# Selective-scan block and coupled feed-forward on one core: the product u moved from GpSimd to VectorE, four more state-and-C products moved the other way, and a new set of places

## The reference, cut to what matters

```python
xi, res = split(x @ W_in.T + b_in)              # 512 channels each
xi      = silu(causal_conv4(xi) + b_conv)       # depthwise, 4 taps, along the 1024 tokens
delta   = softplus(xi @ W_x[:512].T + b_x)      # 512 channels
B, C    = xi @ W_x[512:].T + b_x                # 16 states each
h[t]    = exp(delta[t] * A) * h[t-1] + delta[t] * B[t] * xi[t]    # 512 channels x 16 states
y       = sum over states of h * C + xi * D
x1      = layernorm(x + (y * silu(res)) @ W_out.T + b_out)
# three cycles: t = net(out); out = out + coupling(t) * twist(out); then layernorm(x1 + out)
```

## Time and profile before

| | value |
|---|---|
| median of 3 runs | 4040.12 us |
| profiled execution | 4040.28 us, span 4038.5 us |
| GpSimd busy | 3644.6 us, 90% |
| TensorE busy | 3524.4 us, 87%, granted clock 0.946 over the span |
| VectorE busy | 3429.6 us, 85% |
| ScalarE busy | 2959.0 us, 73% |
| DMA queue of SyncE | 47.0% of 16 engines' span |

### The profile page before, as it was taken

The page is one execution under the profiler, slowest core; times in us unless marked ns, Lnnn a source line. Parts: engine busy times, 40 slices in busy tenths (PEclk is TensorE's granted clock), DMA queues, the critical chain, the costliest instruction groups (busy, mean ns, idle before and its releaser), DMA issues. The chain is left out here.

```text
span 4038.5 us, 51729 instructions
## 1 busy us (share of the span) xinstructions
PE 3524.4 (87%) x18776; PEld 1611.5 (40%) x18776; DVE 3429.6 (85%) x2508; ACT 2959.0 (73%) x3918; POOL 3644.6 (90%) x1604
## 2 busy tenths in 40 slices
PE   7669989899998998989898998989989898897766
PEld 3224353443434344353443434344353443434233
DVE  4988988889898898989889898898989889898861
ACT  4447868778786877868777786877868777785753
POOL 4999999999999999999999999999999999999860
PEclk9779999999999999999999999999999999998888
DMA  5354373543536354373644546454363544546320
GB/s 182 130 175 154 128 230 120 188 152 130 186 130 224 129 191 138 122 229 120 197 148 155 159 152 200 140 187 129 133 218 123 194 149 158 160 138 199 127 86 31
DMA packets 329645, 630.04 MB, mean 156 GB/s; under 512 B 27952, under 2 KB 226608, under 8 KB 329136
## 3 DMA queue, kind: packets, MB, share of 16 engines
q1 hardware_dynamic: 329392, 626.74, 47.0%
HBM read 456.76 MB, written 169.87 MB: 155 GB/s over the span
## 5 line engine op out<-in xcount | busy, mean ns | idle before, releaser
L1060 POOL TENSOR_TENSOR work<-u_q,b_quad 128x1024 f32<-128x1024 f32 x1024 | 2397.3, 2372 | 138.2 <-DMA u_q<-u_scratch 97.1
L816 ACT ACTIVATE da<-delta_q,neg_a 128x1024 f32<-128x1024 f32 x1024 | 1126.3, 1112 | 600.9 <-DVE work L995 430.8
L987 DVE TENSOR_TENSOR_SCAN da<-da,work 128x1024 f32<-128x1024 f32 x608 | 1389.9, 2286 | 151.4 <-ACT da L816 119.7
L1067 POOL TENSOR_TENSOR work<-work,c_quad 128x1024 f32<-128x1024 f32 x416 | 985.2, 2368 | 11.6 <-DVE work L987 11.3
L987 DVE TENSOR_TENSOR_SCAN work<-da,work 128x1024 f32<-128x1024 f32 x416 | 945.9, 2278 | 29.9 <-ACT da L816 28.1
L727 PE MATMUL y_sum<-work,v_all 128*32 128x256 f32 x8192 | 613.3, 399 | 303.3 <-POOL work L1067 190.7
L995 DVE TENSOR_TENSOR work<-da,c_quad 128x1024 f32<-128x1024 f32 x608 | 743.9, 1224 | 28.6 <-DMA c_quad<-bc_scratch 4.6
L752 ACT ACT_TABLE_LOAD x563 | 722.3, 1283 | 14.5 <-DMA v_all<-in_vectors 3.9
L727 PEld LDWEIGHTS y_sum<-work,v_all 128*32 128x32 f32 x8192 | 199.8, 110 | 771.0 <-issue 259.3
L613 PE MATMUL banks<-xi,w_all 128*128 128x512 f32 x1024 | 479.8, 612 | 9.4 <-ACT g_act L797 5.1
L600 PE MATMUL banks<-xi,taps 128*128 128x512 f32 x984 | 453.2, 606 | 0.0
(11 more groups left out here) (86 smaller groups left out, 3270.3 us busy)
## 6 DMA issues: line engine op xcount, KB each, us to landing
delta_q<-delta_scratch SPq DMA_DIRECT2D x256, 512.0 KB, 5.8
u_q<-u_scratch SPq DMA_DIRECT2D x256, 512.0 KB, 6.1
delta_scratch<-delta SPq DMA_DIRECT2D x64, 512.0 KB, 2.9
u_scratch<-soft SPq DMA_DIRECT2D x64, 512.0 KB, 2.9
b_quad<-bc_scratch SPq DMA_DIRECT2D x64, 512.0 KB, 4.7
c_quad<-bc_scratch SPq DMA_DIRECT2D x64, 512.0 KB, 7.1
s_quad<-res_scratch SPq DMA_DIRECT2D x128, 256.0 KB, 4.1
y_scratch<-s_quad SPq DMA_DIRECT2D x128, 256.0 KB, 3.2
```

What stands on the lines that cost most here:

```text
L816: act.activation(da[:, t % 2, :], delta_q[:, slot, :], ACT.Exp, scale=neg_a[:, t % PERIOD:t % PERIOD + 1]).then_inc(da_ready, 1)
L987: dve.tensor_tensor_scan(dst, da[:, t % 2, :], work[:, slot, :], 0.0, ALU.mult, ALU.add) \
L1060: pool.tensor_tensor(work[:, slot, :], u_q[:, copied, :], b_quad[:, j, :], ALU.mult) \
L1067: pool.tensor_tensor(work[:, un % WORK, :], work[:, un % WORK, :], c_quad[:, un % PHASE, :], ALU.mult) \
```

## The change

- `u` is made by VectorE, behind each half of delta (128 x 512, twice a block), with both inputs in SBUF. `store_u` waits for both halves. GpSimd's instruction L1082 goes.
- `POOL_AT` has 30 units instead of 26, most of them others than before. VectorE makes 34 products of a batch instead of 38.
- The first convolution: VectorE makes blocks 0, 1, 2 and a half of block 3, TensorE one half.
- New places for nearly all side work; `DELTA_AT`, `BC_AT`, `G_AT` and `CYCLE_AT` stay.

```diff
-POOL_AT = (1, 4, 6, 8, 9, 10, 11, 12, 16, 18, 21, 24, 28, 32, 33, 36, 42, 44, 49, 52, 55, 56, 58, 59, 60, 61)
+POOL_AT = (0, 1, 4, 8, 9, 10, 12, 13, 16, 17, 20, 22, 25, 26, 28, 32, 33, 37, 38, 42, 45, 46, 48, 49, 52, 56, 57, 59, 60, 61)
-X_AT = (0, 0, 19, 24, 37, 37, 45, 49)
-V_AT = (2, 3, 27, 29, 41, 41, 53, 52)
-RES_AT = (0, 1, 26, 26, 36, 39, 47, 50)
+X_AT = (0, 1, 18, 24, 37, 37, 40, 48)
+V_AT = (2, 2, 28, 28, 41, 42, 52, 50)
+RES_AT = (0, 1, 26, 27, 36, 39, 46, 51)
-O_AT = (5, 9, 10, 12)
-T_AT = (15, 15, 15, 15)
+O_AT = (4, 10, 11, 12)
+T_AT = (15, 15, 15, 16)
-F_AT = (-1, 0, 1, 2, 4, 5, 6, 9, 10, 10)
+F_AT = (0, 0, 0, 2, 4, 5, 6, 8, 10, 10)
-E_AT = (57, 58, 59, 61)
+E_AT = (58, 58, 60, 61)
-DELTA_TAKE, DELTA_MAX, U_LAG = 3, 3, 6
+DELTA_TAKE, DELTA_MAX = 3, 3
-MULT_AT, UPD_AT = 11, 14
-DST_AT, UST_AT = (7, 5, 10, 8), (11, 5, 8, 9)
-DLD_AT, ULD_AT = (12, 13, 18, 19), (12, 13, 17, 20)
-SLD, YST = -1, 0
-YGLD_AT = (2, 4, 4, 8)
-RESST_AT = (4, 28, 47, 61)
-X1ST_AT = (15, 16)
-RES_IN_AT = 28
-XRES_AT = 66
+MULT_AT, UPD_AT = 11, 15
+DST_AT, UST_AT = (8, 10, 6, 9), (8, 4, 4, 8)
+DLD_AT, ULD_AT = (12, 12, 15, 18), (9, 15, 12, 18)
+SLD, YST = 2, -1
+YGLD_AT = (1, 7, 7, 8)
+RESST_AT = (8, 33, 46, 61)
+X1ST_AT = (12, 17)
+RES_IN_AT = 36
+XRES_AT = 70
-XFEAT_AT = 48
-BCST_AT = 54
-LB_AT, LC_AT = (59, 55, 57, 63), (61, 62, 61, 63)
-SILU_AT = (8, 32, 45, 55)
+XFEAT_AT = 47
+BCST_AT = 51
+LB_AT, LC_AT = (54, 54, 56, 57), (58, 62, 63, 63)
+SILU_AT = (8, 31, 45, 55)
-BY_VECTOR, BY_TENSOR = ((0, SEQ), (1, SEQ), (2, L)), 3
+BY_VECTOR, BY_TENSOR = ((0, SEQ), (1, SEQ), (2, SEQ), (3, L)), 1
@@ store_u
-                sp.wait_ge(u_ready, m + 1)
+                sp.wait_ge(u_ready, 2 * m + 2)
@@ vector, behind each half of delta
+                    dve.wait_ge(delta_ready, 2 * m + half + 1)
+                    dve.wait_ge(xi_ready, 8 * (m // DC) + 2 * (m % DC) + 2)
+                    dve.tensor_tensor(u[:, cols], delta[:, cols], xi[:, (m // DC) % 2, m % DC, cols], ALU.mult) \
+                       .then_inc(u_ready, 1)
@@ gpsimd
-                m, half = delta_at(t, U_LAG)
-                if m is not None and half == 0:
-                    pool.wait_ge(delta_ready, 2 * m + 2)
-                    pool.wait_ge(xi_ready, 8 * (m // DC) + 2 * (m % DC) + 2)
-                    pool.tensor_tensor(u[:, :], delta[:, :], xi[:, (m // DC) % 2, m % DC, :], ALU.mult).then_inc(u_ready, 1)
```

More of the change, by code:

```diff
@@ L75 @@
 BC_TAKE = 3
-DELTA_TAKE, DELTA_MAX, U_LAG = 3, 3, 6
-O_STATS, O_RS, O_NORM = 3, 5, 4
+DELTA_TAKE, DELTA_MAX = 3, 3
+O_STATS, O_RS, O_NORM = 3, 5, -15
 T_TAKE = 3
 GELU1_AT, GELU2_AT, GELU3_AT, GELU4_AT, TANH_AT = 3, 5, 7, 9, 11
-MULT_AT, UPD_AT = 11, 14
-DST_AT, UST_AT = (7, 5, 10, 8), (11, 5, 8, 9)
-DLD_AT, ULD_AT = (12, 13, 18, 19), (12, 13, 17, 20)
-SLD, YST = -1, 0
-YGLD_AT = (2, 4, 4, 8)
-RESST_AT = (4, 28, 47, 61)
-X1ST_AT = (15, 16)
-RES_IN_AT = 28
-XRES_AT = 66
-OUT_AT = (64, 64)
-XFEAT_AT = 48
-BCST_AT = 54
-LB_AT, LC_AT = (59, 55, 57, 63), (61, 62, 61, 63)
-SILU_AT = (8, 32, 45, 55)
-BY_VECTOR, BY_TENSOR = ((0, SEQ), (1, SEQ), (2, L)), 3
-X_FIRST, V_FIRST, RES_FIRST = (0, 0, 1, 1, 2, 2, 3, 3), (-1, -1, -1, -1, 7, -1, 7, 7), (58, 58, 59, 59, 60, 60, 60, 60)
+MULT_AT, UPD_AT = 11, 15
[7 more added lines that the diff above has]
+XRES_AT = 70
+OUT_AT = (64, 64)
+XFEAT_AT = 47
[3 more added lines that the diff above has]
+BY_VECTOR, BY_TENSOR = ((0, SEQ), (1, SEQ), (2, SEQ), (3, L)), 1
+X_FIRST, V_FIRST, RES_FIRST = (0, 0, 1, 1, 2, 2, 3, 3), (-1, -1, -1, -1, -1, -1, 7, -1), (58, 58, 59, 59, 60, 60, 60, 60)
 SILU_FIRST, RES_TAKE_FIRST = (8, 9, 10, 11), 3
@@ L897, in _ @@
                             table(SILU)
-                            if nb == 0 and m < 2:
+                            if nb == 0 and m < DC - 1:
                                 act.wait_ge(conv_step, TAPS * m + TAPS)
@@ L905, in _ @@
                             else:
-                                act.wait_ge(conv_ready, 1 if m == 2 else BY_TENSOR)
+                                act.wait_ge(conv_ready, BY_TENSOR)
                             for n in (2 * m, 2 * m + 1):
                                 half = 1 - n % 2
-                                if nb == 0 and n == 5:
+                                if nb == 0 and n == 7:
                                     act.wait_ge(conv_step, TAPS * len(BY_VECTOR))
-                                    act.activation(xi[:, 0, 2, 0:L], work[:, 2, 0:L], ACT.Silu, bias=v("b_conv", 2),
+                                    act.activation(xi[:, 0, 3, 0:L], work[:, 3, 0:L], ACT.Silu, bias=v("b_conv", 3),
                                                    scale=1.0).then_inc(xi_ready, 1)
```

## The result

The changed kernel takes 4230.4 us (median of 4 runs, 4227.7 to 4237.7), the kernel before 4038.5 (4 runs on the same chip). The ratio is 1.0479, with a 95% interval of 1.0467 to 1.0492. The forecast was 3946, its range ended at 4090, and even the slower rival said 4100.

A forecast was written before the change was run, and what follows sets the result against it. The prediction took GpSimd, busy 228.0 of a batch's 241 us, as the fullest engine, with gains in its waits. From 4040.3 it took 91 us of waits and 3 of the start: 3946 us, range 3900 to 4090.

The forecast's parts named there:

- the slower rival: VectorE becomes the bound: each u waits for a whole GpSimd instruction or more, 245 us a batch, 4100 us; chance 0.2.
- the price of u: Each 128 x 512 u on VectorE takes 0.7 us, 5.6 us a batch; 3.0 kept for the range.
- The gate's row: VectorE's 128 x 512 gate in the profile, 0.69 us, taken as the nearest row for pricing u.
- its two cases: VectorE's u and GpSimd take turns fairly, 4024 us, chance 0.2; or VectorE becomes the bound, 4100 us, chance 0.2.
- the other case: The first case: u costs 0.7 us on VectorE and GpSimd's waits shrink; 3910 to 3990 us, chance 0.45.
- the five waits: GpSimd's waits at units 28, 56, 0, 36 and 3: 108 us left for 219 in all.
- I let 20 us of the 111 come back: Of 111 us of GpSimd waits removed, 20 return as waits on scans and reduced units; gain 91 us.
- they follow GpSimd: VectorE and TensorE are idle for 25 us of a batch because they follow GpSimd and its waits.
- The 3 us of the start: At the program's start, the new first convolution lets L613 begin at about 33.9 instead of 37.52; 3 us gained.
- the count of instructions: GpSimd's instructions a batch: four u go and four C products come, 98 before and 98 after.
- VectorE's saving from four products: Four products fewer on VectorE give 4 x 1.27 = 5.1 us a batch.
- the signs to look at: Prediction wrong if u's mean exceeds 1.3 us, scan waits pass 50 us, or batches take 240 us with u at 0.7.

The follow-up runs named there:

- u_from_psum: The changed kernel with u made from delta's input in its PSUM bank, softplus left out of u; 4045.1 us, 1.0005 of the kernel before.
- sync_places: The kernel before with only five numbers of SyncE's order changed, for the waits at units 56, 36 and 3; 3996.3 us, ratio 0.9867.
- the shortened kernels: C products over fewer columns: GpSimd's in the kernel before (3992.3 us); GpSimd's (4024.4) or VectorE's (4011.9) in the changed kernel with u from PSUM.
- first_conv: The kernel before with only the first convolution changed (VectorE blocks 0 to 2 and half of 3); 4040.4 us, ratio 0.9993.
- u_alone: The kernel before with only u moved to VectorE, in two halves, 26 products and all old places; 4245.8 us, ratio 1.0498.
- gpsimd_yields: The changed kernel with GpSimd waiting, three units behind each half of delta, until VectorE has made that half of u; 4138.4 us, ratio 1.0245.

## Why the prediction was wrong

**The step that failed first is the price of u.** "I take 0.7, the row it is nearest to" stood where 3.02 us was measured, just at the upper end of 3.0 that was kept "for the range". The gate's row was the wrong neighbour: of the same size, but one of its inputs is in PSUM. The page "SBUF — State Buffer" of the Trainium skill, section "SBUF: two separate sides", said so: its rule is for two SBUF inputs. The prediction told the rule, gave its two cases 0.4 together and took the other case. Ordinary turns and the lengthened GpSimd instruction agree with that page (2.83 us for 2.37); that VectorE, while it waits, can be passed by instructions that GpSimd begins later (up to four here) it doesn't say.

**The slower rival had the mechanism and too small a price.** "Each u waits for a whole one or more: 8 x 2.3 = 18.4 us a batch" is exact: the excess was 2.33 a piece, 18.6 a batch. But it went on from 214 + 18 to 245 us a batch, and a batch takes 254 (mean of the last 14, from first B product to first B product; 248 to 261). It let all but 12 us of VectorE's idle time absorb the loss. Between the same marks VectorE was idle 28 us a batch before and still 22 in the changed kernel (means of 15), most of it behind ScalarE and TensorE: nearly two thirds of the 298 us came through.

**The second step that failed is "the five waits".** Each single forecast was fair: the waits at units 28, 36, 56 and 3 for delta, u_q and B rows went, and at unit 0 there were 2.5 us in u_from_psum (4.5 forecast). "I let 20 us of the 111 come back" was the error. In u_from_psum all came back: 112 us behind scans and 38 for a free slot, where the prediction had 20 for both, and 37 for u_q at unit 16, where it had seen nothing. Even in sync_places, where only waits were taken away, 53 of 92 us came through. The premise behind it was that VectorE and TensorE are idle because "they follow GpSimd". In the kernel before VectorE waited 31 us for GpSimd's products, but 148 for ScalarE's exponentials and 111 for TensorE's sums. GpSimd, 228 of 241 us busy, looked like the bound because its waits were few and named. A batch is a loop through all four engines with 7 slots of work and 2 of da, and its length follows each engine in part. That is argued from the waits; what the shortened kernels show is the shares.

**The 3 us of the start** were nothing. L613 began at 34.25 us in the changed kernel (forecast 33.9), but its first B product at 61.09, 0.7 later than before, and first_conv can't be told from the kernel before.

**Right** were the count of instructions (98 and 98), VectorE's saving from four products, the start of L613, and the signs to look at: a mean of u over 1.3 us, waits behind scans over 50 us.

**What stays open.** Which of the new places make the set of 26 products cost 116 us more than the set of 30 (1.0292 and 1.0005), what decides whether VectorE gets the first turn or the fifth, and whether the lower granted clock adds to the loss.

## What to carry to other kernels

Before a product moves to VectorE beside a busy GpSimd, look where its two tensors lie: with both in SBUF it costs the rest of a GpSimd instruction and sometimes several, with one in PSUM it costs its own length. Price such an instruction from a row with the same memories, not from one with the same size, and where there is none, let the range's unpleasant end be the forecast. Here a loop of four engines, each 78 to 95% full, gave back a fifth to a bit over half of what was taken off an engine or its waits; count on no more without a run. Try the order of the queue first: five numbers of SyncE's order gave 1.3%, more than any move of work here.

## What the runs showed of the hardware

- A 128 x 512 product of two SBUF tensors on VectorE: 0.69 us where no GpSimd instruction ran (5 cases in the changed kernel, 19 in u_alone, 55 in gpsimd_yields). Over all 128 of the changed kernel, nearly all beside a GpSimd that multiplies SBUF tensors, 2.29 at the median and 11.45 at the most (12.77 in u_alone). With one tensor in PSUM 0.69 in all 128.
- The waiting isn't fair: up to four GpSimd instructions were begun in front of a waiting VectorE (five, once, in u_alone). Stopping GpSimd for it by a semaphore brought the mean from 3.02 to 1.26 us and the kernel from 4230 to 4138.
- The time that u waits is inside its own bar. No idle time stands before it (4.4 us in all), so the table of waits is silent; only the duration tells.
